# A Mamba-style scan on one core: x spread over the states in f32, sums over the states in pairs of scans, and no barrier ahead of the scan

## The reference, cut to what is computed

```python
Bm = sequence @ W_B.T + b_B                                   # (4096, 16)
Cm = sequence @ W_C.T + b_C
Delta = jax.nn.softplus(sequence @ W_Delta.T + b_Delta + bias_Delta)
A_bar = jnp.exp(A[None, None] * Delta[..., None])             # (4096, 256, 16)
B_bar = 1.0 / A * (A_bar - 1.0) * Bm[..., None, :]
...
state = state * Ab + x[..., None] * Bb                        # each token: (256, 16)
y = jnp.einsum('bdn,bn->bd', state, c)                        # sum over the 16 states
...
x = x + _L0_attn_a_ref(_layernorm(x, axis=-1), ...)
x = x + _L0_ffn_ref(_layernorm(x, axis=-1), ...)
x = x + _L0_attn_b_ref(_layernorm(x, axis=-1), ...)
x = x + _L0_ffn_ref(_layernorm(x, axis=-1), ...)
```

## Time and profile before

| | |
|---|---|
| median of 3 runs (lowest, highest) | 3477.95 us (3476.05, 3478.55) |
| profiled execution, its own time | 3478.46 us |
| span of the profiled execution | 3476.6 us |
| mean granted clock of PE, as a share of full speed | 0.988 |
| norm stage, to the barrier | 0 to 77 us |
| scan stage, first to last scan | 83.5 to 595.5 us |

### The profile page before, as it was taken

One profiled execution on the slowest core, in us unless ns is written; L12 is line 12 of the kernel. 1 busy time (PEld: TensorE's weight loads), 2 busy tenths in 40 slices (PEclk: granted clock), 3 DMA queues, 4 the chain that ended last, 5 costly groups with the idle time before them and its releaser, 6 DMA issues.

```text
span 3476.6 us, 59741 instructions
## 1 busy us (share of the span) xinstructions
PE 3330.3 (96%) x22826; PEld 1192.6 (34%) x22852; DVE 3260.1 (94%) x4960; ACT 2718.5 (78%) x4991; POOL 830.4 (24%) x707
## 2 busy tenths in 40 slices
PE   6788888989999999999999999999999999999999
PEld 3222222542333333333333333333333333333334
DVE  7899999589999999999999999999999999999943
ACT  6766665756888888888888888888888888888865
POOL 3899998662000000000000000000000000000004
PEclk9999999988999999999999999999999999999999
DMA  2000001052020120202020202112020202020011
GB/s 65 1 10 0 1 1 49 31 149 30 6 33 13 28 30 10 33 6 33 8 33 6 33 6 33 25 16 33 6 33 6 36 6 33 6 33 6 8 55 49
DMA packets 53678, 87.11 MB, mean 25 GB/s; under 512 B 13200, under 2 KB 40464, under 8 KB 49232
## 3 DMA queue, kind: packets, MB, share of 16 engines
q1 hardware_dynamic: 53200, 82.77, 12.6%
q10 hardware_dynamic: 192, 0.52, 0.1%
HBM read 53.37 MB, written 21.23 MB: 21 GB/s over the span
## 4 chain that ended last, share of the span: by engine, by line
PE 81%; DVE 10%; issue 4%; POOL 1%; ACT 1%; DMA 0%; DVEq 0%; SPq 0%; POOLq 0%; ACTq 0%
PE banks L1493 29%; PE banks L1450 16%; PE banks L1445 15%; PE banks L1408 11%; DVE arena L999 5%; PE banks L553 3%; DVE arena L969 3%; PE banks L1406 2%; PE banks L805 1%; DVE arena L1666 1%; DVE arena L980 1%; PE banks L797 1%; PE banks L1515 1%; POOL arena L1122 0%; POOL arena L1113 0%
## 5 line engine op out<-in xcount | busy, mean ns | idle before, releaser
L1649 DVE TENSOR_REDUCE arena<-banks 128x1 f32<-128x512 f32 x4032 | 2503.7, 683 | 19.1 <-PE banks L1408 15.5
L1623 ACT ACTIVATE arena<-banks 128x512 f32<-128x512 f32 x4096 | 2114.9, 602 | 417.0 <-PE banks L1445 409.5
L1445 PE MATMUL banks<-arena 64*128 64x512 bf16 x4032 | 1245.8, 379 | 0.0
L1450 PE MATMUL banks<-arena 35*128 35x512 bf16 x4032 | 1207.2, 378 | 0.6 <-DMA arena<-max_rows 0.4
L1493 PE MATMUL banks<-arena 128*32 128x512 f32 x8192 | 1090.8, 605 | 0.0
L1406 PE MATMUL banks<-arena 64*128 64x512 bf16 x2048 | 789.2, 387 | 22.9 <-DVE arena L1666 20.2
L1408 PE MATMUL banks<-arena 64*128 64x512 bf16 x2048 | 786.9, 386 | 0.6 <-DVE arena L1649 0.6
L1445 PEld LDWEIGHTS banks<-arena 64*128 64x128 bf16 x4032 | 375.8, 93 | 391.7 <-PE banks L1450 5.7
L1408 PEld LDWEIGHTS banks<-arena 64*128 64x128 bf16 x2048 | 188.2, 93 | 796.6 <-DVE arena L1649 792.4
L1450 PEld LDWEIGHTS banks<-arena 35*128 35x128 bf16 x4032 | 358.0, 93 | 157.7 <-ACT arena L1623 8.7
L1373 POOL TENSOR_TENSOR arena<-arena 64x512 f32<-64x512 f32 x64 | 81.2, 1268 | 1191.6 <-DMA arena<-arena 1157.2
(11 more groups left out here) (137 smaller groups left out, 1730.7 us busy)
## 6 DMA issues: line engine op xcount, KB each, us to landing
arena<-qk_parts SPq DMA_DIRECT2D x242, 128.0 KB, 7.1
qk_parts<-arena SPq DMA_DIRECT2D x32, 384.0 KB, 2.6
arena<-arena SPq DMA_DIRECT2D x63, 128.0 KB, 2.3
x_res<-in_x SPq DMA_DIRECT2D x8, 512.0 KB, 7.9
arena<-in_trig SPq DMA_DIRECT2D x2, 2048.0 KB, 9.0
arena<-qk_parts SPq DMA_DIRECT2D x64, 64.0 KB, 10.9
att_t<-arena SPq DMA_DIRECT2D x128, 32.0 KB
arena<-att_t SPq DMA_DIRECT2D x8, 512.0 KB, 5.5
```

The lines of the kernel that those rows point to most:

```text
L1445: return nc.tensor.matmul(sc[:, (4 * t + j) % SB, :], k, q, start=(j == 1), stop=(j != 1))
L1450: return nc.tensor.matmul(sc[:, (4 * t + j) % SB, :], k, q, start=(j != 1), stop=(j == 1))
L1623: nc.scalar.activation(prob[:, t % PBUF, j * CH:(j + 1) * CH], sc[:, n % SB, :], ACT.Exp, scale=SCALE).then_inc(exp_done, 1)
L1649: nc.vector.tensor_reduce(part_max[:, b % 2, u // NC, u % NC:u % NC + 1], mx[:, unit_bank(b, u), :], AXX, ALU.max).then_inc(dve_read, 1)
```

## The change

- **x is spread in f32.** The turned chunk is kept as `x_t` (f32, written by `copy_turned` directly); the three parts and their instructions (L334, L338, L212, L247) are gone. A spread is 2 f32 products instead of 6 bf16 ones.
- **Sums in pairs.** `channels(n)` orders the tiles so that consecutive scans belong to different groups g = n % 4. The sums of two scans are made together, first the first 512 tokens of both (`sum_pair(n - 1, n, 0)`, at odd n), then, at the next even n behind its spread, the other 512 tokens of both (`sum_pair(n - 2, n - 1, 1)`). `hc` has four buffers.
- **No barrier.** The norm stage's instructions stand in the same block as the scan's. PE makes the first spread ahead of the last chunk's projection; ACT and DVE take parts of the norm stage into the first scans (`outputs(7)` in iteration 0, `minus_abs(3)` behind scan 3). PSUM is one tile for both stages.
- **The start of the scan.** `scan_before` gives two `times_b` behind each of the first scans; u of scan 1 is DVE's; the exponentials of the late quarters are in iteration 6 instead of 5, the sine in 8 instead of 7.

```diff
-    return n % 8 not in BY_DVE and n < NT_SCAN - 1
+    return n % 8 not in BY_DVE and 1 < n < NT_SCAN - 1
...
-    if m < 4:
-        return 0
-    if m < 6:
-        return 1
+    if m < 7:
+        return (m - 1) // 2
     return m - 3 if m > NJH and m % NJH in (7, 8) else m - 4
...
+def channels(n):
+
+    return n % NJ // NJH * NJH + n % 4 * 4 + n % NJH // 4
...
-    hc = place(mem, 152, [2, SC])
+    hc_pairs = (place(mem, 152, [2, SC]), place(mem, 40, [2, SC]))
...
+    def hc(n):
+        return hc_pairs[n // 2 % 2][:, n % 2, :]
+
     def x_bank(n):
 
-        return yb if n in (1, 3) else xr
+        return yb if n in (0, 1, 3) else xr
...
+            c, j = n // NJ, channels(n)
+            if n > 0:
+                pe.wait_ge(w_done, n if n > 3 else max(1, n - 1))
+            if n > NJH and n % NJH == 7:
                 pe.wait_ge(x_added, n // NJH)
             for b in range(SC // CH):
-                for part in range(NPART):
-                    last = nc.tensor.matmul(
-                        x_bank(n)[:, b * CH:(b + 1) * CH], mem.spread[:, j % NJH, :],
-                        mem.xp[:, part, j // NJH, c * SC + b * CH:c * SC + (b + 1) * CH],
-                        start=(part == 0), stop=(part == NPART - 1))
+                last = nc.tensor.matmul(
+                    x_bank(n)[:, b * CH:(b + 1) * CH], mem.spread[:, j % NJH, :],
+                    mem.x_t[:, j // NJH, c * SC + b * CH:c * SC + (b + 1) * CH], start=True, stop=True)
             last.then_inc(xr_ready, 1)
...
-        for n in range(4):
-            spread_x(n)
+        pe.wait_ge(mem.norm.consts, 3)
+        spread_x(0)
+        mem.norm.project(pe, NC - 1)
+        spread_x(1)
+        pe.wait_ge(mem.norm.proj_read, NC)
+        spread_x(2)
+        spread_x(3)
+        pe.wait_ge(mem.norm.gather_step, 5)
+            if n % NJH == 2 and k > 0:
                 turn_y(k, n + 5)
             for m in spreads_before_gather(n):
                 spread_x(m)
-
-            pe.wait_ge(hc_done, n + 1)
-            if n == 0:
-                pe.wait_ge(w_done, 4)
-            if jj == 0 and k > 0:
-                pe.wait_ge(y_copied, k)
-            g, r = jj // 4, jj % 4
-            for b in range(SC // CH):
+            if n % 2 == 1:
+                sum_pair(n - 1, n, 0)
+            elif n > 0:
+                sum_pair(n - 2, n - 1, 1)
+
+        def sum_pair(one, two, b):
+
+            if b == 0:
+                pe.wait_ge(hc_done, two + 1)
+                if two == 1:
+                    pe.wait_ge(w_done, 4)
+                if two % NJH == 1 and two > NJH:
+                    pe.wait_ge(y_copied, two // NJH)
+            for n in (one, two):
+                g, r = channels(n) % NJH // 4, channels(n) % 4
                 last = nc.tensor.matmul(
-                    yb[32 * g:32 * g + 32, b * CH:(b + 1) * CH], mem.gather[:, j, :],
-                    hc[:, n % 2, b * CH:(b + 1) * CH], start=(r == 0), stop=(r == 3),
-                    tile_position=(0, 32 * g))
-            last.then_inc(y_done, 1)
+                    yb[32 * g:32 * g + 32, b * CH:(b + 1) * CH], mem.gather[:, channels(n), :],
+                    hc(n)[:, b * CH:(b + 1) * CH], start=(r == 0), stop=(r == 3), tile_position=(0, 32 * g))
+                if b == 1:
+                    last.then_inc(y_done, 1)
...
+        sum_pair(NT_SCAN - 2, NT_SCAN - 1, 1)
         pe.wait_ge(scan_done, NT_SCAN)
         units.pe_products(pe, 1)
...
-            if n == 5:
+            if n == 0:
+                mem.norm.outputs(act, NC - 1)
+            if n == 6:
                 late_exps()
             if n == 10:
                 late_logs()
-            if n == 7:
-
+            if n == 8:
+                act.wait_ge(mem.norm.angle_step, 10)
                 nc.scalar.activation(mem.w_ffn[:], mem.w_ffn[:], ACT.Sin)
 
...
+            if n % NJ == 0:
+                dve.wait_ge(mem.norm.proj_read, 2 * (n // NJ) + 2)
             nc.vector.tensor_tensor(w[:, n % WBUF, :], x_bank(n), mem.b_rep[:, cols(n)], ALU.mult).then_inc(w_done, 1)
...
         own_u(0)
-        times_b(1)
...
-            ahead = [m for m in range(2, NT_SCAN) if scan_before(m) == n]
+            ahead = [m for m in range(1, NT_SCAN) if scan_before(m) == n]
             own = n + 1 < NT_SCAN and not by_pool(n + 1)
-            if own and len(ahead) == 2:
+            if own and len(ahead) >= 2:
                 times_b(ahead.pop(0))
             if own:
                 own_u(n + 1)
             for m in ahead:
                 times_b(m)
+            if n == 3:
+                mem.norm.minus_abs(dve, NSC - 1)
...
-            if n >= 2:
-                pool.wait_ge(y_done, n - 1)
-            nc.gpsimd.tensor_tensor(hc[:, n % 2, :], st[:, n % 2, :], mem.c_rep[:, cols(n)],
+            if n % NJ == 0:
+                pool.wait_ge(mem.norm.proj_read, 2 * (n // NJ) + 2)
+            if n >= 4:
+                pool.wait_ge(y_done, n - 3)
+            nc.gpsimd.tensor_tensor(hc(n), st[:, n % 2, :], mem.c_rep[:, cols(n)],
...
-        norm_and_project(nc, mem, io)
         mem.banks = ctx.enter_context(nc.psum_tensor("banks", [P, 8, CH], F32))
+        first = norm_and_project(nc, mem, io, ctx)
         middle, last = scan_to_projection(nc, mem, io, ctx), attention(nc, mem, io, out, ctx)
```

478 lines of the change are left out of this document (222 added, 256 removed).

## The result

| | before | after |
|---|---|---|
| median (lowest, highest; executions) | 3477.70 us (3475.70, 3480.62; 20) | 3483.22 us (3479.01, 3496.76; 20) |
| profiled execution, its own time | 3478.46 us | 3479.01 us |
| span of the profiled execution | 3476.6 us | 3477.3 us |
| mean granted clock of PE in it | 0.988 | 0.986 |

The ratio of the times is 1.0024, with a 95% interval of 1.0016 to 1.0031. It lies near that of the means (3486.05 and 3477.70 us), since after has a group of executions near 3495 us; at the medians it is 5.5 us slower, where 3482 was forecast. The profiled execution of after is the fastest of its 20, so its sum closes at +0.55 us of time and +0.7 us of span, and the rest of the 5.5 us has to be looked for in how the executions differ.

What follows compares the result with a forecast made beforehand. DVE was taken to bound the running scan, so gains could only come ahead of it. Terms of -16.1, +0.7, +1.5, +1.2, +3.0, +11.9 and +2.1 sum to +4.3; 3478.46 + 4.3 - 0.5 gives 3482 us, range 3465 to 3496.

Steps and rivals of the forecast that it cites:

- Start, -16.1: Norm stage to scan 4: scan 4 starts at 89.7 instead of 105.79 us, a gain of 16.1 us.
- `minus_abs(3)` beside POOL, +0.7: First scans: this DVE instruction now runs beside POOL and takes longer, +0.7 us (ends 0 and 1.3).
- Clock at the first spreads, +1.5: First scans: PE idles, then an f32 spread at lower clock takes 3.5 us instead of 1.9; +1.5 (ends 0 and 3.5).
- Logarithms and sine, +1.2: Scan stage: ACT's logarithms still delay `decay(11)`, and the slow spread behind that wait grows; +1.2 us (ends 0 and 2.5).
- The spread at each turn, +3.0: Steady scan: DVE's wait for a spread once a turn grows by 0.43 us, seven times; ordinary spreads stay hidden.
- The copy at each turn, +11.9: Each turn: `copy_y` comes 2.9 us later behind the half sums, so DVE waits 1.7 us for `decay`, seven times.
- Clock at the turns, +2.1: Each turn: PE idles 3.3 us ahead of the turning; a lower clock slows it and the next spread; +2.1 (ends 0 and 13).
- One of my signs of being wrong: Scan stage: wrong if the granted clock is at half in more than a few stretches between 100 and 590 us.
- The copy costs nothing: Rival, turns: `copy_y` starts as before or ACT catches up, 11.9 and 2.1 fall away; 3468 us, chance 0.22.
- The pairs don't run side by side: Rival, sums on PE: each half costs 1.9 us instead of 1.05, copy 0.86 later; 3492 us, chance 0.10.
- The spread is too long: Rival, steady scan: room of 0.17 us is too small, 0.1 us over it costs 8 us; 3490 us, chance 0.12.
- The clock falls at every turn: Rival, turns: a full slow spread each time, +11 in place of 2.1; 3493 us, chance 0.15.

Runs made afterwards that it cites:

- e9: The changed kernel itself, run once more without any edit: 3483.53 us, ratio 1.0025 against before; the profiled execution took 3481.98 us.
- e5: The changed kernel with the splitting of chunks 0 to 6 in three bf16 parts put back in the norm stage, results unused: 3494.14 us, ratio 1.0047 against before.
- e6: The changed kernel with the barrier of all engines put back between norm stage and scan stage: 3495.58 us, ratio 1.0047 against before.
- e7: The changed kernel with the order of the first scans as before and u of scan 1 on POOL: 3486.13 us, ratio 1.0016 against before.
- e1: The changed kernel with the last half pair of sums ahead of the spread at each turn, instead of behind it: 3473.53 us, ratio 0.9985 against before.
- e2: The changed kernel with one more ACT instruction, its result unused, behind each copy of a turn: 3493.25 us, ratio 1.0044 against before.
- e8: The changed kernel with six unused f32 products as filler in PE's idle time ahead of each turning: 3490.98 us, ratio 1.0035 against before.
- e3: The changed kernel with each scan's sums made alone, both halves at that scan, instead of in pairs: 3484.43 us, ratio 1.0017 against before.
- e10: The kernel of e1 with spread 4 waiting for three products with B instead of four: 3471.15 us, ratio 0.9981 against before.
- e4: The changed kernel with spreads of six bf16 products again, lower parts of x left out: 3482.57 us, ratio 1.0012 against before.

## Why the prediction came out right

**The forecast, 3482 us; measured 3483.22.** It lies in the range, and the mechanism of the sum (a gain ahead of the steady scan, a loss at each turn) is the one that the profile shows. That it came within 1.2 us is partly luck. The sum was made for the profiled execution and gave +4.3; the two that were profiled have +0.7 and +3.1 (e9) of span, and the median of 20 has +5.5, by executions that no profile caught. Term by term, against the profile of after:

- **Start, -16.1**: -15.85 at scan 4 (89.94 against 105.79), with `minus_abs(3)` in it. That counts the 1.32 us by which the first chunks came earlier; from chunk 1's products on it is -14.53, against -13.9 forecast for this term and the next two together. The split of it was wrong, though. I had 8 us for the norm stage, with PE setting its pace, 2 for the barrier and the rest for the first scans. By the distances it is -17.24 up to scan 0 and +2.71 from there to scan 4, so the first scans lost. Putting the splitting back costs 9.3 us of it (e5), through the queues of DVE and ACT and not PE's; the barrier alone 1.0 at scan 0 and about 2 more by scan 4 (e6); the order of the first scans 3.3 at scan 0 and nothing at scan 4 (e7). At scan 0 that is 13.6 of the 17.24; what the rest is was not tried alone.
- **`minus_abs(3)` beside POOL, +0.7**: 2.49 us instead of 1.20, so 1.3, its upper end.
- **Clock at the first spreads, +1.5**: spreads 4 and 5 were fast in both profiles of after (24.98 us to scan 4) and slow in e1, e2 and e8 (28.50), by 3.5 us, the upper end that I had. Which of the two comes varies behind the same idle time of 3.37 us. The other executions of after may have either; none of the slow kind was profiled.
- **Logarithms and sine, +1.2**: from scan 4 to scan 16, where they lie, 51.04 us instead of 50.28, so +0.76. The 16 scans from 8 on grew by 3.86 us, 1.4 more than a usual turn, but the scans just ahead of them came 0.6 us quicker, with the exponentials moved.
- **The spread at each turn, +3.0**: 0.51 us per turn, +3.6. The f32 spread is 1.98 us long and not 1.90. Its first weight load is open: 191 ns on average against 98 for bf16. The ordinary spreads still fit, as the distance of two `times_b` is 3.37 us as before. The rule of the Trainium skill that I had weighed ("TensorE: Matmul & The Clock Gate", Weight-path perf modes) keeps fast weight load to types other than FP32. By it I had 0.7 us more than the sum; the trace agrees, with 3.6 us.
- **The copy at each turn, +11.9**: a wait of 1.72 us (forecast 1.7) and the 0.1 by which an instruction that waits starts later, 7 x 1.8 = 12.6. e1 takes it away and e2 adds to it, each turn by about the amount that the queue gives.
- **Clock at the turns, +2.1**: the rest of the 2.43 us, 0.1 per turn, 0.7 in all. e8 and e7 confirm that it is small where only the turning is slow.

The three terms of the turns together were forecast at 17.0 us and measured 7 x 2.43 = 17.0; here two misses cancelled.

One of my signs of being wrong did come: the granted clock is at half in nine stretches between 100 and 590 us, against two before. It was badly chosen, since seven of them lie on the turning, which DVE hardly waits for.

**The rivals.** "The copy costs nothing" fell with e1. "The pairs don't run side by side" fell with the groups: 131.5 us for 476 records, 230.9 for 484 with single sums in e3. "The spread is too long" fell with the distance of 3.37 us. "The clock falls at every turn" is half true. In both profiled executions of after it falls at every turn, but ends with the turning (0.2 us behind it in the first turn of e9). In e2 it reached the next spread in every second turn, for 1.2 us, and in e7 two spreads in one turn, for 3.1 us. If it did that in all seven turns, it would be 8 to 22 us (an estimate from these two). The group of executions of after near 3495 us, 15 over the fastest and with a mean granted clock of 0.982 instead of 0.986, fits this. No profile caught one of them, so their cause stays open; without the five near 3495 the median would be 3481.27, so they make half of the 4 us by which it lies over the best. e1, e3 and e10, whose PE is not idle for 3 us at the turns, have none more than 7 us above their lowest; but neither has e4, where it is idle for 3.1 us and more.

## What to carry to other kernels

When work in order on an engine is regrouped, look for the rarest consumer of its result first: one half pair behind a spread instead of ahead of it cost 1.6 us in each turn. That is more than the 1.4 us that the pairs bring beside an f32 spread (e1 against e3), so in after the 99 us that PE saved gave nothing; with the half pair in its place they would have been worth their 1.4 us a turn. Then go through the waits that were written for the old order: one that counted one product too many held PE idle for 3.4 us, and DVE then waited 3.9 us for the spread behind it. And read the start in distances from a fixed event, since the arrival of the first data moves everything behind it by up to 3 us from one execution to the next.
